# A recurrence with interleaved expert products: eight-column gate products, a negated sigmoid, half jobs and one shared PSUM bank

## The reference, cut to what matters

```python
# GRU: h starts as the conditioning vector, one step per token t, all 8 sequences at once
r = sigmoid(x_t @ W_ir + b_ir + h @ W_hr)
z = sigmoid(x_t @ W_iz + b_iz + h @ W_hz)
n = tanh(x_t @ W_in + b_in + r * (h @ W_hn + b_hn))
h = (1 - z) * n + z * h
# experts on the GRU's output y (D_FF = 512): top-1 by router logits, over capacity goes to expert 0
out = relu(y @ W1[e] + b1[e]) @ W2[e] + b2[e]
```

## Time and profile before

| | us |
|---|---|
| median of 3 runs (1581.71 to 1587.13) | 1583.0 |
| the profiled execution, its own time | 1581.07 |
| its span, first to last instruction | 1579.0 |
| PE busy | 1460.8 (93%) |
| PEld busy | 1132.5 (72%) |
| DVE busy | 732.8 (46%) |
| ACT busy | 651.0 (41%) |
| `gru_scan`, from about 449 to 967 on the span's clock | 518 |

### The profile page before, as it was taken

One profiled execution on the slowest core, in us unless ns is written; L12 is line 12 of the kernel. 1 busy time (PEld: TensorE's weight loads), 2 busy tenths in 40 slices (PEclk: granted clock), 3 DMA queues, 4 the chain that ended last, 5 costly groups with the idle time before them and its releaser, 6 DMA issues. The chain is left out here.

```text
span 1579.0 us, 30235 instructions
## 1 busy us (share of the span) xinstructions
PE 1460.8 (93%) x11078; PEld 1132.5 (72%) x11078; DVE 732.8 (46%) x2721; ACT 651.0 (41%) x2429; POOL 106.7 (7%) x141
## 2 busy tenths in 40 slices
PE   7999978999989999999999998799999999767995
PEld 5333324777779999999999996488888888644663
DVE  3576765455433444444444445633333332863223
ACT  2322204565524554554554552134444443622442
POOL 4000000000000000000000000100000000004662
PEclk8999989999999999999999998599999999957998
DMA  5000000000030000000000000100000000001113
GB/s 158 1 0 0 1 0 1 1 1 1 1 108 1 1 2 2 1 2 1 2 1 2 1 2 1 34 21 22 22 22 28 22 2 1 1 27 33 42 43 96
DMA packets 27724, 27.95 MB, mean 18 GB/s; under 512 B 2293, under 2 KB 22234, under 8 KB 27450
## 3 DMA queue, kind: packets, MB, share of 16 engines
q1 hardware_dynamic: 20970, 16.70, 3.6%
q0 software_dynamic: 2496, 5.12, 1.1%
q10 hardware_dynamic: 4112, 4.19, 0.9%
HBM read 21.35 MB, written 4.65 MB: 16 GB/s over the span
## 5 line engine op out<-in xcount | busy, mean ns | idle before, releaser
L1625 PE MATMUL spare<-identb 128*128 128x128 bf16 x3166 | 218.4, 219 | 0.0
L1625 PEld LDWEIGHTS spare<-identb 128*128 128x128 bf16 x3166 | 202.0, 103 | 4.3
L1223 DVE TENSOR_TENSOR_SCAN narg<-rz,pre_n 128x16 f32<-128x16 f32 x256 | 47.9, 187 | 220.2 <-PE pre_n L1120 219.0
L1158 ACT ACTIVATE ghid<-gh_ps,cols 128x128 f32<-128x128 f32 x512 | 144.3, 365 | 12.9 <-PE gh_ps L1059 12.7
L1059 PE MATMUL gh_ps<-hist,w 128*128 128x128 f32 x1024 | 137.5, 275 | 0.6 <-ACT ghid L1158 0.6
L1068 PE MATMUL gy_ps<-w2e,ghid 128*128 128x128 f32 x1024 | 136.8, 276 | 0.8 <-DVE g_diff L1204 0.3
L1068 PEld LDWEIGHTS gy_ps<-w2e,ghid 128*128 128x128 f32 x1024 | 124.4, 191 | 3.2 <-issue 3.2
L1059 PEld LDWEIGHTS gh_ps<-hist,w 128*128 128x128 f32 x1024 | 125.9, 188 | 0.8 <-DVE hist L1231 0.8
L1144 ACT ACTIVATE rz<-pre_r 128x8 f32<-128x8 f32 x256 | 45.6, 178 | 181.9 <-PE pre_r L1120 179.2
L1120 PE MATMUL pre_r<-hist,gru_w 128*128 128x128 f32 x512 | 118.1, 311 | 0.8 <-DVE hist L1231 0.5
L1676 DVE TENSOR_TENSOR_SCAN targ<-gates,pairs 128x16 f32<-128x16 f32 x256 | 49.1, 192 | 140.8 <-ACT gates L1635 140.8
(11 more groups left out here) (412 smaller groups left out, 2516.4 us busy)
## 6 DMA issues: line engine op xcount, KB each, us to landing
w<-in_L_ffn_W SPq DMA_DIRECT2D x1, 2048.0 KB, 9.6
raw<-in_L_ffn_wg SPq DMA_DIRECT2D x8, 256.0 KB, 3.0
raw<-in_L_ffn_wu SPq DMA_DIRECT2D x8, 256.0 KB, 2.8
raw<-in_L_ffn_wd SPq DMA_DIRECT2D x8, 256.0 KB, 2.7
wqkv<-in_L_attn_Wqkv SPq DMA_DIRECT2D x1, 1536.0 KB, 6.6
mrow<-mt SPq DMA_DIRECT2D x4, 256.0 KB, 2.4
y_top<-yrow SPq DMA_DIRECT2D x4, 256.0 KB, 5.4
y_next<-yrow ACTq DMA_DIRECT2D x4, 256.0 KB, 5.8
```

The costliest lines, as they stand in the source:

```text
L1158: nc.scalar.activation(hid[v % 2][:, f, :], h_ps[:, f, :], ACT.Relu, bias=n.cols[:, at:at + 1]).then_inc(h_done, 1)
L1223: V.tensor_tensor_scan(narg[p][:, :], rz[p][:, 0:16], n_slot(s), 0.0, ALU.mult, ALU.add).then_inc(narg_done, 1)
L1625: nc.tensor.matmul(spare[:, 0:P], n.identb[:, :], n.identb[:, :], start=True, stop=True)
```

## The change

The diff touches `gru_scan` alone.
1. The r and n products take `now`, the 8 columns of the current state, and write 8 columns. The z product stays at 128.
2. The z sigmoid has scale -1 and gives `fresh` = 1 - z. One DVE instruction, `(fresh - 1) * h` = -z * h, takes the place of `keepz` and `mix`. The tanh has scale -1 and gives -n. The state scan subtracts its addend instead of adding it, s = a * s - b, which turns both signs back: n in the first column, (1 - z) * n + z * h in the second.
3. A job is cut in halves: in every step PE issues two `hidden` products (four passes), then a small product if there is one, then two `output` products. `gh_ps` uses two quarters of its bank; the other two are `turn_ps` and `diff_ps`, and the logits are 8 columns in `turn_ps`. `gy_ps` has a bank for itself.
4. The small products move to k = 0 (logits, 8 columns), 1 (turning back), 3 (choice) and 5 (b2). DVE reads them in the same step, in `turned`, ahead of the state scan; ACT's Relus in those steps wait until DVE has read. `add` follows one job, not two, behind.
5. The 16 logits products of the tail stand in one block at s = T, and the loop has 274 turns.

```diff
-        h_ps = ps("gh_ps", [P, NF, P])
-        y_bank = ps("gy_ps", [P, 4, P])
-        y_ps, turn_ps, diff_ps, logits_ps = (y_bank[:, i, :] for i in range(4))
+        h_bank = ps("gh_ps", [P, 4, P])
+        h_ps, turn_ps, diff_ps = h_bank[:, 0:2, :], h_bank[:, 2, :], h_bank[:, 3, :]
+        logits_ps = turn_ps[:, 0:E]
+        y_ps = ps("gy_ps", [P, 512])[:, 0:P]
...
-        STEPS = T + G + 5
+        HALVES = 2 * JOBS
+        STEPS = T + G + 2
...
+                def hidden(u):
+                    v, half = divmod(u, 2)
+                    grp, e = divmod(v, E)
+                    if u == 0:
+                        pe.wait_ge(n.load_experts, 32)
+                    else:
+                        pe.wait_ge(h_done, 2 * u)
+                    for f in (2 * half, 2 * half + 1):
+                        mm = nc.tensor.matmul(h_ps[:, f % 2, :], w1[:, e, P * f:P * f + P], tokens(grp), start=True, stop=True)
                     mm.then_inc(h_in, 1)
...
+                def output(u):
+                    v, half = divmod(u, 2)
+                    e = v % E
+                    pe.wait_ge(h_done, 2 * (u + 1))
+                    if half == 0 and v:
                         pe.wait_ge(summed, v)
+                    for f in (2 * half, 2 * half + 1):
                         mm = nc.tensor.matmul(y_ps, hid[v % 2][:, f, :], w2[:, e, f, :], start=(f == 0), stop=(f == NF - 1))
+                    if half:
+                        mm.then_inc(y_in, 1)
...
+                    grp, k = divmod(s - G, G)
+                    if s - G < HALVES:
+                        hidden(s - G)
+                    if k == 0 and grp < GROUPS:
+                        nc.tensor.matmul(logits_ps, tokens(grp), n.cols[:, r0:r0 + E], start=True, stop=True).then_inc(logits_in, 1)
+                    if k == 1 and grp:
+                        pe.wait_ge(summed, E * grp)
                         nc.tensor.transpose(diff_ps, diff[:, :], n.ident[:, :])
                         nc.tensor.transpose(turn_ps, y0[:, :], n.ident[:, :]).then_inc(back_in, 1)
+                    if k == 3 and grp < GROUPS:
+                        pe.wait_ge(choosing, 4 * (grp + 1))
                         nc.tensor.transpose(turn_ps[0:E, :], choice[:, :], n.ident[:, :]).then_inc(choice_in, 1)
+                    if k == 5 and grp < GROUPS:
+                        pe.wait_ge(choice_kept, grp + 1)
                         nc.tensor.matmul(turn_ps, n.b2[:, :], choiceT[:, :], start=True, stop=True).then_inc(bias_in, 1)
+                    if 0 <= s - G - 1 < HALVES:
+                        output(s - G - 1)
...
-                        for out, i, ready in ((r_out, 3, r_pre), (n_out, 5, n_pre), (z_out, 4, z_pre)):
-                            nc.tensor.matmul(out, n.gru_w[:, i, :], h, start=False, stop=True,
+                        for out, i, rhs, ready in ((gate_slot(pre_r, s), 3, now, r_pre), (first(n_slot(s)), 5, now, n_pre),
+                                                   (z_out, 4, h, z_pre)):
+                            nc.tensor.matmul(out, n.gru_w[:, i, :], rhs, start=False, stop=True,
                                              skip_group_check=True).then_inc(ready, 1)
                     elif s == T:
                         pe.wait_ge(state, T + 1)
+                        for m in range(NBLK):
+                            b, half = divmod(m, SEG)
+                            states = hist[:, 16:16 * (T + 1)].rearrange("p (t b two) -> p two b t", b=B, two=2)[:, 1]
+                            mm = nc.tensor.matmul(pre_r[0][:, E * m:E * m + E], states[:, b, P * half:P * half + P],
+                                                  n.cols[:, r0:r0 + E], start=True, stop=True)
+                        mm.then_inc(all_logits, 1)
...
-                        nc.scalar.activation(second(rz[s % 2][:, 16:32]), gate_slot(pre_z, s), ACT.Sigmoid).then_inc(z_done, 1)
+                        nc.scalar.activation(second(fresh[s % 2][:, :]), gate_slot(pre_z, s), ACT.Sigmoid, scale=-1.0).then_inc(z_done, 1)
                         act.wait_ge(narg_done, s + 1)
-                        nc.scalar.activation(first(mix[s % 2][:, :]), second(narg[s % 2][:, :]), ACT.Tanh).then_inc(n_done, 1)
+                        nc.scalar.activation(first(mix[s % 2][:, :]), second(narg[s % 2][:, :]), ACT.Tanh, scale=-1.0).then_inc(n_done, 1)
...
+                    u = s - G
+                    if 0 <= u < HALVES:
...
+                        if k == 0:
+                            act.wait_ge(choosing, 4 * grp + 2)
+                        if k == 1 and grp:
+                            act.wait_ge(kept, 2 * grp)
+                        if k == 3:
+                            act.wait_ge(choice_kept, grp + 1)
+                        if k == 5:
+                            act.wait_ge(bias_kept, grp + 1)
                         if v >= 2:
                             act.wait_ge(y_in, v - 1)
+                        for f in (2 * half, 2 * half + 1):
...
+                def turned(s):
+
+                    grp, k = divmod(s - G, G)
+                    if k == 0 and grp < GROUPS:
+                        choose(grp, 0)
+                        choose(grp, 1)
+                    if k == 1 and grp:
+                        keep(grp - 1)
+                    if k == 3 and grp < GROUPS:
+                        dve.wait_ge(choice_in, grp + 1)
+                        V.tensor_copy(choiceT[:, :], turn_ps[0:E, :]).then_inc(choice_kept, 1)
+                    if k == 5 and grp < GROUPS:
+                        dve.wait_ge(bias_in, grp + 1)
+                        V.tensor_copy(diffT[:, P * grp:P * grp + P], turn_ps).then_inc(bias_kept, 1)
...
-                        V.tensor_scalar(second(keepz[p][:, :]), z, -1.0, 1.0, ALU.mult, ALU.add).then_inc(z_used, 1)
-                        V.tensor_tensor(second(mix[p][:, :]), z, second(at_step(s)), ALU.mult).then_inc(z_used, 1)
-                        dve.wait_ge(z_used, 2 * s + 2)
+                        V.scalar_tensor_tensor(second(mix[p][:, :]), second(fresh[p][:, :]), 1.0, second(at_step(s)),
+                                               ALU.subtract, ALU.mult).then_inc(mixed, 1)
+                    if s >= G:
+                        turned(s)
+                    if s < T:
+                        dve.wait_ge(mixed, s + 1)
                         dve.wait_ge(n_done, s + 1)
-                        V.tensor_tensor_scan(at_step(s + 1), keepz[p][:, :], mix[p][:, :], 0.0,
-                                             ALU.mult, ALU.add).then_inc(state, 1)
+                        V.tensor_tensor_scan(at_step(s + 1), fresh[p][:, :], mix[p][:, :], 0.0,
+                                             ALU.mult, ALU.subtract).then_inc(state, 1)
...
+                    if k == 1 and grp < GROUPS:
+                        choose(grp, 2)
+                        choose(grp, 3)
+                    v = (s - G) // 2 - 1
                     if k % 2 == 0 and 0 <= v < JOBS:
                         add(v)
```

More of the change, by code:

```diff
@@ L981, in gru_scan @@
         pre_n = [ps(f"pre_n{i}", [P, 512]) for i in range(2)]
-        h_ps = ps("gh_ps", [P, NF, P])
-        y_bank = ps("gy_ps", [P, 4, P])
-        y_ps, turn_ps, diff_ps, logits_ps = (y_bank[:, i, :] for i in range(4))
-        rz = [sb(f"rz{i}", [P, 32]) for i in range(2)]
+        h_bank = ps("gh_ps", [P, 4, P])
+        h_ps, turn_ps, diff_ps = h_bank[:, 0:2, :], h_bank[:, 2, :], h_bank[:, 3, :]
+        logits_ps = turn_ps[:, 0:E]
+        y_ps = ps("gy_ps", [P, 512])[:, 0:P]
+        reset = [sb(f"reset{i}", [P, 16]) for i in range(2)]
         narg = [sb(f"narg{i}", [P, 16]) for i in range(2)]
-        keepz = [sb(f"keepz{i}", [P, 16]) for i in range(2)]
+        fresh = [sb(f"fresh{i}", [P, 16]) for i in range(2)]
         mix = [sb(f"mix{i}", [P, 16]) for i in range(2)]
@@ L1052, in inputs @@
                     nc.tensor.matmul(out, lhsT, rhs, start=(i < 3), stop=False, skip_group_check=True)
[L1054 to L1065 removed]
+                def hidden(u):
[7 more added lines that the diff above has]
+                        mm = nc.tensor.matmul(h_ps[:, f % 2, :], w1[:, e, P * f:P * f + P], tokens(grp), start=True, stop=True)
+                    mm.then_inc(h_in, 1)
+                def output(u):
[3 more added lines that the diff above has]
+                    if half == 0 and v:
                         pe.wait_ge(summed, v)
[L1067 removed]
+                    for f in (2 * half, 2 * half + 1):
                         mm = nc.tensor.matmul(y_ps, hid[v % 2][:, f, :], w2[:, e, f, :], start=(f == 0), stop=(f == NF - 1))
[L1069 removed]
+                    if half:
+                        mm.then_inc(y_in, 1)
                 def work(s):
[L1072 to L1073 removed]
+                    if s < G:
                         for _ in range(FILL):
@@ L1111, in _ @@
                         h = second(hist[:, 16 * s:16 * (s + G)]).rearrange("p (s b) -> p s b", b=B)
```

(32 more changed lines are left out.)

68 lines of the change are left out of this document (11 added, 57 removed).

## The result

The changed kernel takes 1620.2 us (median of 4 runs, 1615.04 to 1629.71) beside 1582.36 before; the ratio is 1.026, with a 95% interval of 1.0215 to 1.0305. It is slower, as forecast, but by 38 us where 15.6 were worked out, and outside the range. The profiled execution took 1620.38 us, with a span of 1618.3.

What follows compares the result with a forecast made beforehand. The z path, not PE, was taken to end the plain step. Body +5.0, tail +9.0 and the tail's lower clock +1.6 gave +15.6 us on 1581.1, stated as 1597, with a range of 1584 to 1611.

Steps and rivals of the forecast that it cites:

- The plain step: Recurrence step without input, bias or small product: 1.72 us falls to 1.63, ended by the z path.
- (a): Rival: narrow passes cost some 0.025 us instead of 0.11, relieving PE in every step; kernel takes 1526; 6%.
- (d): Rival: the fused DVE instruction costs as much as the two, no gain in plain steps, 1604; 10%.
- The four stalls: Steps 0, 1, 3 and 5 of a group wait for PE's small product: 2.21, 2.35, 1.98 and 2.28 us.
- Input steps: Three steps a group with wide input products, 16 PE passes, set by PE: 1.82 us falls to 1.80.
- bias steps: Four steps a group carrying a bias product, set by PE: 2.18 us falls to 2.16.
- special steps: Recurrence steps in which the state scan waits for a small product, counted as 61 and known to 0.1 us.
- The tail: From last state scan to next function: 26.4 us grows to 35.4, +9.0, plus 1.6 for a lower clock.
- the ring: In the tail, each of 16 expert halves runs as a closed PE-ACT loop of 1.43 us, PE idle some 0.5.
- The first group: First 16 recurrence steps, with filler and no small products: nine plain steps at -0.09, seven at -0.02, -0.9 us.
- Rival (c): PE idles about a third of steps 0 and 1, the clock falls in each group: 63 us, 1660; 4%.
- Rival (b): Unchanged within 4.7 us: the four special steps cost 0.15 less each, tail clock holds, 1586; 15%.

Runs made afterwards that it cites:

- e4: The changed kernel with the 16 logits products of the tail one a turn, as before, instead of in one block: 1614.4 us, 1.0203 of before.
- e8: The changed kernel with r and n wide in the first 16 steps and the tail's logits one a turn: 1592.1 us, 1.0065 of before.
- e1: The changed kernel with r and n back on 128 columns in all steps: 1601.6 us, 1.0132 of before.
- e2: The changed kernel with r and n on 128 columns in the first 16 steps alone: 1607.7 us, 1.0164 of before.
- e6: The changed kernel with 32 filler products instead of 16 in each step of the first group: 1612.9 us, one run.
- b2: The kernel before with the negated sigmoid and fused DVE instruction, and bias products of 128 rows instead of one: 1551.3 us, 0.9799 of before.
- b3: As b2, and the product of the turned choice and b2 (the bias) with 128 rows instead of 8: 1543.4 us, 0.9756 of before.
- b1: The kernel before with the negated sigmoid and fused DVE instruction, and r, z and n biases given to ACT: 1569.0 us, 0.9927 of before.

## Why the prediction was wrong, point by point

- **The plain step: right.** 1.63 forecast, 1.64 measured; the z path still ends it, the fused instruction lasts 0.17, and narrow passes give PE 0.01 a step. Rivals (a) and (d) are out. The r and n pairs are 0.21 apart at full clock. The Trainium skill's "TensorE: Matmul & The Clock Gate" gives this spacing in "LDWEIGHTS (loading the stationary operand)", with 107 ns a load, and does not in the table of "Back-to-back issue gap". At half clock, though, the two loads of a narrow pair are 0.21 apart, twice what that section on LDWEIGHTS gives.
- **The four stalls: right.** 0.60, 0.72, 0.36 and 0.66 measured, 0.58, 0.72, 0.35 and 0.65 forecast. Input steps 1.80 (1.80) and bias steps 2.18 (2.16). A group costs +0.61, not +0.47, mostly by those 0.02. Three slips of the sum matter little. There are 60 special steps in the 256, not 61. The last bias product of a group stands behind step 15's work and so lengthens step 0 of the next group (2.18 before, 2.78 after): a full group's sum is the same, but the last group takes 28.9 before and 29.0 after, not 28.4. And the second group, set against 30.54 and forecast at -0.2, took 30.1 before and 30.5 after.
- **The tail: right in kind, a little small.** 11.7 against 10.6; the block is 6.9 (6.8) and the ring 1.44 (1.43). The clock fell in the block of narrow passes as put, and stayed down for 13.7 us, which by e4 cost 2.1 where 1.6 were put.
- **The first group: this step failed.** It was put at "nine plain steps at -0.09 and seven at -0.02: -0.9"; it is +14.1. The sum has no term for the clock there. The clock was read from the page as a given of the stretch ("so durations there are comparable"), not as a product of what PE does in it, although the same prediction gave few columns a price in the tail; and the half clock with which the kernel before enters the group was left out.
- **The clock in later groups: put at nothing in the sum.** Rival (c) had it in every group, at 63 us and 4%. It came in few, the clearest in the fifteenth group, which takes 35.3 instead of 31.15. The profile of the changed kernel shows 3.4 and 10.2 us at 1.2 GHz there, 4.9 us of time by e8. Both begin in step 1, so the place is rival (c)'s, PE idle in steps 0 and 1; but e1 has the same stalls and no such stretch, so idle time alone was not enough. The rest of the 8.6 by which these groups missed is 1.8 from the 0.14 a group in thirteen groups, 0.8 in the second and the last, and 1.1 left over, in the groups with one longer step. Rival (b) leaned on a clock that holds; it did not.
- **Sum.** 15.6 + 15.0 (first group) + 8.6 (further groups) + 1.1 (tail) is 40.3; the stages around give back 1.0. The direction was not luck: with the first group's clock mended the kernel is still slower (e1, e2), by the stalls and the tail that the prediction had worked out. The span grew by 39.3.

## What to carry to other kernels

Before making a product narrower, ask what its streaming was doing besides its own work: here 120 of 128 columns were zeros and cost 0.01 us a step, since the weights took as long, and without them the clock was not raised for 37.5 us. Where two engines wait for the same read, moving one wait moves little. And where a stage is bound by the count of products, look at those with few rows: a product of 1 or 8 rows made its step 0.38 longer than one of 128 rows did, and padding these with zeros was worth 31 us.

## What the runs showed of the hardware that was not expected

- PE counted busy for 37.50 of 37.50 us stays at 1.2 GHz when four of its six recurrent passes stream 8 columns; with wide ones (e1), or with 32 fillers instead of 16 (e6), the level changes after 6.8 us. The Trainium skill ("TensorE: Matmul & The Clock Gate", Part 1) has activity release a throttled clock; the runs agree, but what the profile calls busy is not that activity.
- The same work can run for long at either level. In e4 the second group stays at 1.2 GHz for its first 13.1 us (503.2 to 516.3), while the second group of the changed kernel, with the same passes, runs at 2.4 GHz throughout (36.3 and 30.5 us).
- A product of 1 row, and one of 8, makes its step 0.38 longer than the same with 128 rows (2.18 to 1.80, b2 and b3). What PE does in that time no run shows.
- A bias column adds 0.09 to an ACT activation of 8 columns (178 to 268 ns, 202 to 291 ns, b1).
